# Preparing the channel mix's first batch inside the last batch of the softmax attention

## What is computed

```
x = x + cosine_attention(layernorm(x), ctx)
x = x + ternary_ffn(layernorm(x))
x = x + softmax_attention(layernorm(x), ctx)     # 16 heads of 32 channels
x = x + channel_mix(layernorm(x))
```

```
x_prev = concatenate([zeros, x[:, :-1, :]], axis=1)   # the token before
xr = mu_r * x + (1.0 - mu_r) * x_prev
xk = mu_k * x + (1.0 - mu_k) * x_prev
r = sigmoid(xr @ W_r)
k_act = square(relu(xk @ W_k))
out = r * (k_act @ W_v)
```

## Time and profile before

| | us |
|---|---|
| median of 3 runs | 1814.31 |
| lowest and highest | 1812.78 and 1816.18 |
| the profiled execution's own time | 1815.05 |
| its span, first to last instruction | 1813.2 |
| PE busy in the span | 1600.2 (88%) |
| DVE, ACT, POOL busy | 1231.7, 1158.4, 1095.0 |
| softmax attention | about 677 to 1497 |
| channel mix | about 1499 to the end |

### The profile page before, as it was taken

The page is one execution under the profiler, slowest core; times in us unless marked ns, Lnnn a source line. Parts: engine busy times, 40 slices in busy tenths (PEclk is TensorE's granted clock), DMA queues, the critical chain, the costliest instruction groups (busy, mean ns, idle before and its releaser), DMA issues. The chain is left out here.

```text
span 1813.2 us, 31173 instructions
## 1 busy us (share of the span) xinstructions
PE 1600.2 (88%) x8930; PEld 724.6 (40%) x8930; DVE 1231.7 (68%) x1740; ACT 1158.4 (64%) x1908; POOL 1095.0 (60%) x792
## 2 busy tenths in 40 slices
PE   5799478998999966899999999999999974999998
PEld 2355233443444422343444444444444322444443
DVE  2778778888888664667676767676766636466553
ACT  5476498888888613676666666565657545655662
POOL 3577356888989832575665666574747554455442
PEclk9899789999999976999999999999999986999999
DMA  8221000000000013111120101111101002001001
GB/s 296 96 81 58 1 1 1 1 1 1 0 0 1 1 48 100 46 36 54 29 57 26 57 27 56 32 54 29 58 24 41 26 1 70 24 23 46 23 23 47
DMA packets 60478, 72.30 MB, mean 40 GB/s; under 512 B 14416, under 2 KB 40016, under 8 KB 59856
## 3 DMA queue, kind: packets, MB, share of 16 engines
q1 hardware_dynamic: 56944, 62.22, 10.8%
q10 hardware_dynamic: 3424, 8.91, 1.3%
HBM read 37.40 MB, written 8.39 MB: 25 GB/s over the span
## 5 line engine op out<-in xcount | busy, mean ns | idle before, releaser
L1393 DVE TENSOR_REDUCE s_mx<-bank 128x1 f32<-128x512 f32 x512 | 336.3, 685 | 201.4 <-PE bank L1503 195.6
L1303 ACT ACTIVATE s_E<-bank 128x512 f32<-128x512 f32 x512 | 293.5, 595 | 207.9 <-PE bank L1517 183.2
L1223 POOL TENSOR_TENSOR s_E<-s_E 128x1024 f32<-128x1024 f32 x128 | 299.1, 2356 | 128.9 <-PE bank L1525 121.4
L962 PE MATMUL bank<-f_zh,f_w1q 128*128 128x512 f16 x512 | 200.2, 391 | 38.6 <-DVE f_y L830 35.8
L620 POOL TENSOR_TENSOR f_y<-f_y,f_t 128x511 f32<-128x511 f32 x128 | 173.5, 1357 | 65.2 <-DVE f_y L830 65.2
L1503 PE MATMUL bank<-s_KA,s_QA 96*128 96x512 f16 x512 | 193.2, 388 | 16.4 <-DMA s_KA<-s_qkh 8.7
L963 PE MATMUL bank<-f_zl,f_w1q 128*128 128x512 f16 x512 | 199.5, 390 | 0.0
L1517 PE MATMUL bank<-s_QA,s_KA 97*128 97x512 f16 x512 | 195.6, 383 | 4.0 <-ACT s_E L1303 2.3
L1216 POOL TENSOR_TENSOR s_qkl<-s_qkf,s_qkh 128x512 f16<-128x512 f32 x64 | 76.2, 1190 | 183.9 <-ACT s_qkh L1281 183.1
L1693 POOL TENSOR_TENSOR m_xl<-m_xf,m_xh 128x512 f16<-128x512 f32 x64 | 90.4, 1421 | 112.2 <-ACT m_xh L1736 112.2
L1525 PE MATMUL bank<-s_E,s_V 128*32 128x512 f32 x1024 | 137.0, 607 | 2.6 <-ACT s_E L1303 2.6
(11 more groups left out here) (238 smaller groups left out, 3842.4 us busy)
## 6 DMA issues: line engine op xcount, KB each, us to landing
X<-in_x SPq DMA_DIRECT2D x8, 1024.0 KB, 6.9
s_QA<-s_qkh SPq DMA_DIRECT2D x256, 32.0 KB, 1.8
out_x<-X SPq DMA_DIRECT2D x8, 1024.0 KB, 4.3
s_KA<-s_qkh SPq DMA_DIRECT2D x248, 32.0 KB, 1.9
a_cf<-in_ctx SPq DMA_DIRECT2D x8, 768.0 KB, 5.1
s_cf<-in_ctx SPq DMA_DIRECT2D x8, 768.0 KB, 4.7
w1raw<-in_w ACTq DMA_DIRECT2D x1, 4096.0 KB, 13.5
w2raw<-in_w ACTq DMA_DIRECT2D x1, 4096.0 KB, 29.7
```

Source lines behind the costliest of these rows:

```text
L962: e.matmul(hb(odd, j), w1q[:, cols], zh(odd, c), start=(c == 0), stop=False)
L1223: e.tensor_tensor(into, into, other, ALU.add).then_inc(s_sum.sem, 1)
L1303: e.activation(E[:, SLOT[k] + h, :], SC[u % 2][:, :], ACT.Exp, scale=1.0 / float(np.sqrt(DH)))\
L1393: e.tensor_reduce(mx[:, q, h:h + 1], MX[q % 2][:, :], AX.X, ALU.max).then_inc(s_red.sem, 1)
```

## The change

Rooms of SBUF are now shared by the two layers: `zz` (attention `zh` and `zl`, then channel mix `zf`), `cx` (context parts and `qkh`, `qkl`, then `xh` and `xl`), `wq` (then W_k's parts), `wkv` (then W_r's parts), `mu`, `omu`. Inside the attention, the idle query and key tiles `QA` and `KA` serve as staging room for the raw weights and for `part` and `xf`. With this:

- in batch 7, steps 0 and 1 hold the layer norm of the channel mix's batch 0 (as "batch 8"), and step 1 its 16 transposes, read out by ACT (`shifted`) into `zf`;
- step 3 of batch 7 splits W_k on DVE at unit 1, and makes mixes 0 to 3; the tail makes mixes 4 to 7 between its output blocks, and splits W_r: ACT after its last mix, DVE after the last residual;
- the channel mix starts with keys(0). W_v alone is loaded and split in it, beside keys(0) and gates(0); the semaphores that belong to batch 0's preparation are credited in full;
- for all batches, the last transposed chunk moves from unit 11 to 10, and two of step 1's four reciprocals from units 8 and 10 to 7 and 9.

```diff
-    T_UNITS, STATS_UNITS = (4, 6, 8, 11), (1, 3, 6, 10)
+    T_UNITS, STATS_UNITS = (4, 6, 8, 10), (1, 3, 6, 10)
+    MIX_UNITS, XF_UNITS = (2, 4, 8, 10, 13), (3, 5, 9, 11)
-    RC_UNITS, AN_UNIT = ({14: (0, 1, 2, 3)}, {8: (0,), 10: (1,), 12: (2,), 13: (3,)}, LATE_RC, LATE_RC), 14
+    RC_UNITS, AN_UNIT = ({14: (0, 1, 2, 3)}, {7: (0,), 9: (1,), 12: (2,), 13: (3,)}, LATE_RC, LATE_RC), 14
...
@@ block.sync
+                if last and m == 2:
+                    e.wait_ge(s_sc.sem, s_sc.count(b, 16 * 2))
+                    e.dma_start(raw_k..., wkk_d...).then_inc(s_raw[0], 16)
...
+            e.wait_ge(s_raw[2], 16)
+            e.dma_start(mu[:, 0:KD], muk_d).then_inc(s_raw[2], 16)
+            e.dma_start(mu[:, KD:2 * KD], mur_d).then_inc(s_raw[2], 16)
             steps(step, e)
+            e.wait_ge(s_sc.sem, s_sc.count(B - 1, 16 * NG))
+            e.dma_start(raw_r..., wr_d...).then_inc(s_raw[1], 16)
...
@@ block.gpsimd
+            def mixed(i):
...
+                s_xh.wait(e, 0, i + 1)
+                e.tensor_tensor(xl[:, i, :], xf[i % 3], xh[:, i, :], ALU.subtract).then_inc(s_xl.sem, 1)
...
                 summed(b, m, 0, 0)
                 summed(b, m, 0, 1)
+                if last and m == 3:
+                    mixed(0)
+                    mixed(1)
...
             steps(step, e)
+            mixed(2)
+            mixed(3)
             for q in range(TT):
...
+            for i in range(KD, 2 * KD):
+                mixed(i)
@@ block.scalar
+            def mix(i):
+                if i < 2 * KD:
+                    c = i % KD
...
+                    s_zh.wait(e, B, c + 1)
+                    s_xf.wait(e, 0, max(i - 1, 0))
+                    e.activation(part[i % 2], zf[:, c, 0:S], ACT.Copy, scale=omu[:, i:i + 1]).then_inc(s_part.sem, 1)
+                if i:
+                    s_xf.wait(e, 0, i)
+                    e.activation(xh[:, i - 1, :], xf[(i - 1) % 3], ACT.Copy).then_inc(s_xh.sem, 1)
...
                     exponential(b, m, u)
+                    if last and m == 3 and u in MIX_UNITS:
+                        mix(MIX_UNITS.index(u))
...
+            for i in range(KD + 1, 2 * KD + 1):
+                mix(i)
+            e.wait_ge(s_raw[1], 32)
...
+            e.activation(mixed_h[1][0], raw_r, ACT.Copy, scale=WS).then_inc(s_hi, 1)
@@ block.vector
+            def mix(i):
+                s_part.wait(e, 0, i + 1)
+                s_xl.wait(e, 0, max(i - 2, 0))
...
+                e.scalar_tensor_tensor(xf[i % 3], zf[:, i % KD, 1:S + 1], mu[:, i:i + 1], part[i % 2],
+                                       ALU.mult, ALU.add).then_inc(s_xf.sem, 1)
...
+            mix(KD)
             for q in range(TT):
+                if q:
+                    mix(KD + q)
                 residual(B - 1, q, (R6, R7)[q % 2])
+                if q == TT - 1:
+                    e.wait_ge(s_hi, 5)
...
+                    e.scalar_tensor_tensor(mixed_h[1][1], raw_r, WS, mixed_h[1][0], ALU.mult, ALU.subtract)
...
@@ channel_mix
-            ln_t(e, 0, T, s_zf)
-            e.wait_ge(s_lo, 1)
             step(0, False, True)
```

More of the change, by code:

```diff
@@ L1241, in step @@
                 e.tensor_tensor(tile(b, m), tile(b, m), bo[:, :], ALU.add).then_inc(s_bo.sem, 1)
-                if m == 0 and not last:
+                if m == 0:
                     ln_p(e, b + 1)
@@ L1433, in step @@
                             moments(e, b + 1)
-                    if m == 1 and not last and u < TT:
+                    if m == 1 and u < TT:
                         normalise(e, b + 1, (u,))
@@ L1584, in step @@
                         maximum(*nxt, u + MAX_AHEAD)
-                    if m == 1 and not last and u in T_UNITS:
-                        transposed(b + 1, T_UNITS.index(u))
+                    if m == 1 and u in T_UNITS:
+                        transposed(b + 1, T_UNITS.index(u), last)
                     if proj and u in K_UNITS[m]:
@@ L1753, in gate, with step @@
                 e.activation(r[:, q, :], RB[q % 2][:, :], ACT.Sigmoid, scale=1 / WS).then_inc(s_r.sem, 1)
-            def step(b, last):
+            def step(b, last, first=False):
                 keys(b)
@@ L1758, in step @@
                     transposed(b + 1)
+                if first:
+                    wa(e)
                 for q in range(TT):
@@ L1765, in step @@
                         mix(b + 1, i)
-            e.wait_ge(s_c, 2)
-            wa(e, (0,))
-            transposed(0)
-            for i in range(2 * KD + 1):
-                mix(0, i)
-            wa(e, (1, 2))
-            step(0, False)
+            step(0, False, True)
             batches(e, 1, B - 1, lambda b: step(b, False))
```

139 lines of the change are left out of this document (93 added, 46 removed).

## The result

The changed kernel takes **1787.71 us** (median of 4 runs, 1785.34 to 1789.07) where the kernel before took 1814.95 beside it (4 runs, 1812.78 to 1816.18): a ratio of 0.985, interval 0.9833 to 0.9867. Four more runs, in another group, gave 1788.73 (1785.45 to 1789.74), ratio 0.9858 (0.983 to 0.9885). The forecast was 1790.3, in a range of 1786.5 to 1797.0. The profiled execution took 1788.65, with a span of 1786.3; before, the span was 1813.2, so the two profiles differ by 26.9 us. First the page after: span, the busy time of the engines, and the granted clock in 40 slices.

A forecast was written before the change was run, and what follows sets the result against it. PE was taken to bound middle batches, with 21.4 us at the layers' seam, all but the hand-over uncovered preparation. Terms -6.5 +1.85 +4.7 +3.3 -19.35 -8.0 gave -24.0: 1791.05 profiled, 1790.3 median; range 1786.5 to 1797.

The forecast's parts named there:

- D: End of the attention's tail: chain of third residual, mix 7, `xh` 7 and W_r's two parts; +3.3 us, bounds 0 and +4.5.
- E: Head of the channel mix: preparation gone, keys(0) follow the attention's end after 1.88 plus 0.15 us; -19.35 us.
- F: From keys(0) to gates(0): batch 1's layer norm covered by keys(0), gates(0) no longer at low clock; -7.5 and -0.5 us.
- C: Step 3 of batch 7: ACT and POOL bound; longer lists and DVE/POOL collisions delay the last denominators; +4.7 us, bounds +3.3, +8.
- A: Unit tables, batches 0 to 6: PE's 8.0 us wait before values goes, a new 0.15 us wait each; -6.5 us.
- B: Steps 0 and 1 of batch 7: 16 transposes on a busy PE, the rest covered; +1.85 us, at most +2.96.
- no collision: Lower bound for step 3 of batch 7, without DVE's mixes and POOL excluding each other: +3.3 us; with collision +4.6.
- Rival 1: Attention batches: the tables give nothing, PE waits at the transposes instead of the values; 1796.8 us, chance 0.10.
- rivals 3 and 4: 3: preparation stays on the path before keys(0), 1807 us, chance 0.03; 4: moved reciprocals slow batches, 1821 us, chance 0.02.
- Rival 2: Step 3 of batch 7 and the tail cost more, through in-order waits and a fallen clock; 1795.5 us, chance 0.12.
- rival 5: Tail: PE stays at the lower clock through all 48 output matmuls, +7.6 us; 1798 us, chance 0.04.

The follow-up runs named there:

- second profile of the changed kernel: The changed kernel run again with no edit, in another group beside the kernel before: 1788.73 us, ratio 0.9858.
- filling alone: 15 unread PE products in the tail's idle time, added to the changed kernel with W_k load later, W_r split later, POOL's list reordered: 1784.04 us.
- the last kernel: Against the filled kernel: ACT makes W_r's high part behind its first two banks of keys(0), and POOL's last `X+bo` returns to step 3; 1780.23 us.

## Why the prediction came out right, and where it did not

The profiles differ by 26.9 us where the sum said 24.0. D and E came as they were worked out, and F within 0.7; C was 2.5 us too dear and the tail gave 1.2 that nobody had counted, and against these stands a DMA wait of 1.1 that was not foreseen. That the total lies so near is in part these errors cancelling.

**A, the tables: -6.5 predicted, -6.1 measured.** The gain of 1.0 to 1.1 us in each of batches 1 to 6 is there, and the new wait of 0.15 us for bank 7 is not: the rows that showed DVE idle ahead of the residual were the right ones. What was wrong is batch 0: its wait of 1.34 went, but the one for DVE's maxima is 0.73 in place of 0.34, one of 0.20 for a low part is new, and two waits without a named releaser are 0.8 longer together; the batch is 0.16 longer. I had counted seven equal batches. With the tables as the only difference it is 6.7 to 7.4, as above.

**B, the transposes: +1.85 predicted;** 1.64 measured; A had taken 1.1 off in batch 6 and the DMA wait had added 1.13, which leaves 1.6 for B. Right.

**The DMA wait, +1.1 to +1.3, was not foreseen.** "The two issues of 1 MB on SP (nothing is queued behind them that anyone waits for)" looked at SP's queue alone. The small DMA on ACT's queue was beside it, not behind it, and was late.

**C, step 3: +4.7 predicted; +3.3 with the same slow start, +2.2 in the profile, +0.9 in the changed kernel's second one.** The mechanism is right, POOL's longer list with collisions in it, and the terms on POOL are too: two low parts 2.2 (2.4), mix 2 on the first pair 0.45 (0.65), mix 3 on `X+bo` 0.4 (0.7). What failed is ACT's 0.7, which I added to POOL's delay: POOL's first pair began only 0.2 later. That the +3.3 equals my lower bound "no collision" is luck, since the collisions are in it. The rest is the clock: before, PE began the step at the lower level (1.77), after it at the upper (1.06). I had taken the step of before as a warm one.

**The tail: nothing predicted, -1.23 measured.** 6 of its output matmuls were slow (0.6 us instead of 0.38) in place of 12; in the second profile of the changed kernel it was 12 again, and the stretch 13.38, so it varies from run to run of one kernel.

**D: +3.3 predicted, +3.12 measured,** by the chain as it was written, and confirmed by taking it away. **E: -19.35 and -19.52.** Right, with the hand-over of 1.88 us to the hundredth; the 0.15 for a first weight load didn't show.

**F: -7.5 predicted, -6.78 measured.** No wait for `z`, as forecast; the transposes take 3.71 (3.75 forecast). What was off is the clock's part: 13 slow matmuls of keys(0) in this profile, where I took the ten of before; in the other kernels 7 to 9, 8 of them in the changed kernel's second profile (15.89 us from keys(0) to gates(0), -7.7). The -0.5 for gates(0) is right.

**Not the change's doing: -1.6 in the channel mix,** where the profile of before has one batch with a slow stretch (36.75 us instead of 35.10), and +0.7 ahead of batch 0. Such a stretch stands somewhere behind gates(0) in 11 of the 14 profiles, the changed kernel's second among them (gates(0) to the end 270.4 us; 268.8 in the three without).

Rival 1 was shown false; rivals 3 and 4 did not come. Rival 3's price was wrong, too: without E and half of F, 23.4 us are lost by the terms above, not 17, so it stood for 1813.7. Rival 2's clock and rival 5's were real in kind: a slow stretch costs 1 to 3 us (1.6 in the channel mix, 2.8 in step 2). That such stretches are what makes the runs of one kernel differ by 4 us fits these sizes, but is not shown, since of the 4 or 5 runs of a kernel only one has a trace.

## What to carry to other kernels

Where work is moved ahead of a block's end, follow each engine's list to its end: here the moved split of W_r made a new end of 3.1 us, most of which the next block could hide. When PE waits only at a few places, remove the waits together, since one that is left is met earlier and, as here, the clock can fall behind it: filling alone gave nothing, filling with the wait gone (and one POOL step put back) 1.9 us by the traces and 3.4 by medians of different groups. Issue a large load after the small transfer that an engine is about to wait for, even if the two are on different queues. When two experiments are compared in a stretch, compare the level of PE's clock at its start and at its end first: here it moved the stretch by as much as the edits did.

## What the runs showed of the hardware

- A 1 MB load on SP's queue held a small DMA on ACT's queue, and PE with it, by 1.0 to 1.4 us in all seven profiles in which it was ahead, and in none of the five in which it was behind.
- PE idle for 1.1 to 1.4 us was followed by 6.7 us at 1.2 GHz in some executions and by none in others of the same kernel; 7 to 13 slow matmuls of keys(0) followed the end of the attention, where PE stood idle for 2.8 to 5.9 us, in every kernel with the moved preparation but the filled one, whose first 24 matmuls behind 3.25 us of idle time were fast; 7 were slow also in the last kernel, where PE had been idle for 2.05 us only; there they began 1.4 us after the restart. The Trainium skill, "TensorE: Matmul & The Clock Gate", section "Why this matters for your kernels", advises against gaps between bursts; no run here shows how short a gap would be safe.
- DVE's product-and-subtract on 128x2048 took 2.29 us alone and 4.32 beside POOL; a POOL subtraction 1.15 and 3.21; a mix of 8 columns on DVE 0.23 and 1.30.
- The first half of the split on DVE, 128x2048 from 32 to 16 bits without a second SBUF input, took 1.43 us, where the half with two took 2.29; the two POOL sums beside it took 5.65 instead of 4.67.
- The next block's first instructions began 1.88 us behind the last instruction of the block before, in the kernel before and in the changed one.
